# New program orders for all five engines in a fused convolution, attention and expert kernel

## The chip, the cores and the metric

The kernel runs on one core of a Trainium2 chip. The metric is the device time of one execution in microseconds (us). The kernel before took 2512.27 us (median of three runs, 2511.83 to 2513.58).

## What is computed

The input is a batch of 32 images of 56 x 56 positions with 32 channels. Three layers follow each other, each added to its input. The helpers are cut out here.

```python
x = x + conv(group_norm(x))            # batch norm, sign, 3 x 3 convolution with sign(W) * mean|W|
t = tokens(x)                          # 3136 tokens of 32 channels per image
t = t + attention(layer_norm(t))       # 16 heads of 32, linear attention:
    q, k = elu(x Wq + b) + 1, elu(x Wk + b) + 1;  v = x Wv + b
    kv_cos = sum_s k cos(pos) v;  kv_sin = sum_s k sin(pos) v
    qkv = q cos(pos) kv_cos + q sin(pos) kv_sin
    denom = 1 / (q cos(pos) . sum_s k cos(pos) + q sin(pos) . sum_s k sin(pos) + 1e-5)
    out = (qkv * denom) Wdense + b
t = t + experts(layer_norm(t))         # router softmax over 8 experts, the best 2, weighted sum
```

## The kernel before

A prologue (up to about 95 us) loads weights and tables and computes the statistics of the norms over the whole batch. Then the 32 images run through a software pipeline. One image is split into 7 tiles of 4 x 112 positions; each piece of work on a tile or a pair of tiles is a *step*, named by a kind and a number.

Every engine runs its own endless sequence of steps. That sequence isn't derived by the program: it is a table, `ORDER` (line 115), with a list of times for each engine and kind, in units of which `PERIOD = 14` make one image. `iteration` (line 190) sorts all times modulo the period and turns the whole periods into an image offset: a step with time 20.5 is done in iteration i for image i - 1. `walk` (line 216) runs the iterations -3 to B + 2 and calls the engine's `step` function. Only the sorted sequence counts; the numbers themselves play no further part. Each engine takes its steps strictly in this sequence, and steps wait for each other on semaphores.

The steps of one image, with the lines in which the profile shows them:

- **XT**: load (SP, L445), transpose (TensorE L516), sign into `nat` (VectorE L921), residual (ScalarE L663). **CV**: SP copies four shifted versions (L458), convolution (TensorE L525), VectorE L929 adds the residual.
- **XC, SM1, PN1, ZT**: first layer norm. TensorE centres (L530), ScalarE copies and squares (L671, L672), SM1 on VectorE sums the squares (L937) and makes the variance (L940), PN1 on GpSimd takes the power -0.5 and multiplies (L775, L779), TensorE transposes (L537), ScalarE and VectorE split the result into two halves of 16 bits (L679, L951), and SP copies it 16 times into `z` (L465).
- **K** (14 steps): TensorE L546, exponential on ScalarE L683, VectorE L955. **KX** (14): TensorE L555 accumulates keys against positions times values; CS on GpSimd (L787) makes its other operand; KT on ScalarE (L692) and **G** (L564, L696, L701) turn the sum into the matrices for queries.
- **Q** (14): TensorE L571, ScalarE L688, VectorE L961. **DN** (8 steps, VectorE L970 after the 4th and the 8th), **SU** (L588, ScalarE L706), **RC** (VectorE L973, ScalarE L710 and L712), **RL** (VectorE L978): the denominators.
- **R** (7) and **RP** (7): TensorE L597 spreads the denominators; R is multiplied into the queries by VectorE (L983), RP goes through ScalarE (L718) to GpSimd (L792). **NM** (7): TensorE L606, VectorE L989. **T2** (4): TensorE L617 and L619, ScalarE L728 and L730, GpSimd L797.
- **S2, SM2, PN2, ZU**: second layer norm with the same lines as the first (S2: L736 and L945). **LG, RT, GT**: router (TensorE L625, VectorE L993 to L1038, GpSimd L806 to L811). **F** (7): experts, TensorE L631, VectorE L1045, GpSimd L821 to L827. **OUT**: GpSimd L815, store by SP (L472).

PSUM sets how far TensorE may run ahead. K, R, RP, Q, G, LG, F, XC, ZT and ZU share a ring of three slots of two banks (`RING`, `RING_SLOTS = 3`): a step may only start once the step three places before it in TensorE's own sequence has been read. XT, CV, DN, SU, NM and T2 share a single bank (`MISC`), KX has the eighth bank to itself. `rounds` (line 203) works these slots out from TensorE's sequence, so they change with it. The matmuls of K, Q, R and RP write results of 112 or 128 columns, KX, NM and SU of 64, DN and G of 32.

Of the kernel before, what the change touches and what calls it, by code (L numbers as in the profile page):

```python
# [16 lines left out]
G = 4  # L17
# [75 lines left out]
class Img:  # L93
# [10 lines left out]
    def par(self):  # L104
# [9 lines left out]

ORDER = {
    "tensor": {
# [17 lines left out]
    },  # L134
    "vector": {
# [17 lines left out]
    },  # L153
    "scalar": {
# [15 lines left out]
    },  # L170
    "gpsimd": {
        "F": [36.50, 36.53, 37.45, 39.74, 39.75, 42.92, 43.62],
        "PN2": [29.03],
        "RP": [12.84, 15.28, 15.78, 16.42, 17.76, 18.46, 21.18],
        "PN1": [-11.38],
        "CS": [-11.36, -3.38],
        "OUT": [45.32],
        "T2": [18.02, 21.36, 22.75, 26.09],
        "GT": [32.56],
    },  # L180
    "sync": {
        "XT": [-41.70],
        "ZU": [20.02],
        "OUT": [34.22],
        "ZT": [-19.50],
        "CV": [-28.62],
    },
}

# [910 lines left out]
```

How the kernel before makes its waits and increments, by code:

```python
        def wait(eng, s, v):  # L400
            if not isinstance(v, int) or v > 0:
                eng.wait_ge(s, v)
# [10 lines left out]
        @block.sync  # L413
        def _(sp):
            sp.dma_start(eye_center[:, :], eyec).then_inc(eye_in, 16)
            x4 = x.rearrange("(q b) h w c -> q b (h w c)", b=4).rearrange("q b (p f) -> q p b f", p=PT)
            for k in range(2):
                sp.dma_start(stage[k], x4[k]).then_inc(stage_in[k], 16)
            for dst, src in ((mean4_sb[:, :], mean4), (views["rows"], conv_rows),
                             (small[:, 0:1], gamma), (small[:, 1:2], beta), (small[:, 2:3], wd_b)):
                sp.dma_start(dst, src).then_inc(consts_in, 16)
            for q in range(2, 8):
                sp.wait_ge(stage_turned, 4 * q - 4)
                sp.dma_start(stage[q % 2], x4[q]).then_inc(stage_in[q % 2], 16)
            for dst, src in ((views["taps"], conv_taps), (views["valid"], validc), (wva_s, wv[0]), (wvb_s, wv[1]), (wd_s, wd),
                             (views["wqa"], wq[0]), (wqb_s, wq[1]), (views["wka"], wk[0]), (wkb_s, wk[1]),
# [20 lines left out]
            def step(kind, m, n, rd):  # L447
                if kind == "XT" and n == 0:
                    wait(sp, xres_made, m.at(2))
                    load(m)
                if kind == "CV" and n == 0:
                    sp.wait_ge(binarized, m.at(2, 2))
                    for g in range(G):
                        dy, dx = g // 2, g % 2
                        q = slice(32 * g, 32 * g + 32)
```

## Time and profile before

| | |
|---|---|
| median of 3 runs | 2512.27 us |
| the profiled execution, its own time | 2511.5 us |
| its span, first to last instruction | 2509.7 us |
| TensorE busy | 2271.0 us, 90% |
| VectorE busy | 2175.7 us, 87% |
| GpSimd busy | 1745.9 us, 70% |
| ScalarE busy | 1560.4 us, 62% |
| mean granted TensorE clock over the span | 0.964 |

The busy times are unions of the recorded instructions. A busy TensorE isn't a TensorE at its peak, since a matmul's record covers the whole of its passage. The page also follows back the chain of work that ended last: 60% of the span on it is TensorE, 23% VectorE, 9% issue, 3% GpSimd, 2% ScalarE.

### The profile page before, as it was taken

What the parts mean: (1) busy time and instruction counts of PE and PEld (TensorE: products, weight loads), DVE (VectorE), ACT (ScalarE), POOL (GpSimd) and SP (SyncE); (2) the same over time, 40 slices, a digit from 0 to 9 for tenths busy, and PEclk for the clock granted to TensorE, in tenths of its full rate; (3) what the DMA queues carried; (4) which work ended last, traced back from release to release, by engine and by line L of the source; (5) the groups of instructions that cost most, each with busy time, mean ns of one, the idle gap of its engine ahead of it and who ended that gap; (6) DMA issues with size and microseconds to landing.
All of it is one profiled execution on the core that took longest, in us unless ns stands there. A gap on an engine that the chain in (4) does not pass through costs nothing.

```text
span 2509.7 us, 45423 instructions
## 1 busy us (share of the span) xinstructions
PE 2271.0 (90%) x15908; PEld 1106.9 (44%) x15908; DVE 2175.7 (87%) x2949; ACT 1560.4 (62%) x2757; POOL 1745.9 (70%) x1425
## 2 busy tenths in 40 slices
PE   4379999999999999999999999999999999999961
PEld 4224444444444444444444444444444444444441
DVE  5358999999999999999999999999999999999962
ACT  0157666667666666667666666676666666676620
POOL 0414577777777787787777777777777877777675
PEclk8579999999999999999999999999999999999985
DMA  8321111222222112122221111222211111211001
GB/s 221 97 36 21 33 33 32 37 36 43 43 43 38 35 33 36 33 43 43 43 43 33 33 34 35 38 43 43 43 36 34 33 37 34 43 37 34 20 20 26
DMA packets 284863, 105.31 MB, mean 42 GB/s; under 512 B 246032, under 2 KB 279680, under 8 KB 284512
## 3 DMA queue, kind: packets, MB, share of 16 engines
q1 hardware_dynamic: 284640, 102.41, 20.7%
q8 instruction: 131, 2.15, 0.4%
q14 instruction: 92, 0.75, 0.1%
HBM read 31.19 MB, written 12.85 MB: 18 GB/s over the span
## 4 chain that ended last, share of the span: by engine, by line
PE 60%; DVE 23%; issue 9%; POOL 3%; ACT 2%; DMA 2%; SPq 1%; POOLq 0%; DVEq 0%; ACTq 0%
PE ps L555 12%; PE ps L606 10%; PE ps L546 7%; DVE qbuf L961 6%; PE ps L580 6%; PE ps L597 5%; PE ps L571 4%; DVE kbuf L955 4%; PE ps L631 3%; DVE prod L1045 2%; DVE rs L978 2%; DVE qbuf L983 2%; PE ps L530 2%; PE ps L537 2%; PE ps L625 2%
## 5 line engine op out<-in xcount | busy, mean ns | idle before, releaser
L792 POOL TENSOR_TENSOR qbuf<-spread_r,qbuf 128x896 f32<-128x896 f32 x224 | 468.7, 2093 | 335.0 <-ACT spread_r L718 335.0
L683 ACT ACTIVATE ebuf<-ps,small 112x1024 f32<-112x1024 f32 x448 | 499.5, 1115 | 306.4 <-PE ps L546 254.9
L955 DVE SCALAR_TENSOR_TENSOR kbuf<-ps,ebuf 112x1024 f32<-112x1024 f32 x448 | 544.1, 1214 | 78.6 <-ACT ebuf L683 70.4
L688 ACT ACTIVATE ebuf<-ps,small 128x896 f32<-128x896 f32 x448 | 451.8, 1008 | 207.5 <-PE ps L571 149.7
L961 DVE SCALAR_TENSOR_TENSOR qbuf<-ps,ebuf 128x896 f32<-128x896 f32 x448 | 484.8, 1082 | 15.8 <-ACT ebuf L688 14.5
L555 PE MATMUL ps<-kbuf,xcs 112*64 112x512 f32 x1792 | 482.4, 617 | 6.3 <-DVE kbuf L955 6.2
L606 PE MATMUL ps<-qbuf,gmat 128*64 128x224 f32 x3584 | 387.8, 358 | 2.6 <-DVE pbuf L989 2.4
L775 POOL TENSOR_TENSOR rstd<-varr,power 112x28 f32<-112x28 f32 x64 | 307.3, 4802 | 74.9 <-DVE varr L940 71.4
L546 PE MATMUL ps<-wk,z 128*112 128x512 f16 x896 | 284.0, 399 | 54.4 <-DVE qbuf L961 33.6
L606 PEld LDWEIGHTS ps<-qbuf,gmat 128*64 128x64 f32 x3584 | 240.5, 137 | 155.6 <-issue 77.2
L1045 DVE TENSOR_TENSOR prod<-ps,gate 112x1024 f32<-112x1024 f32 x224 | 272.5, 1217 | 22.1 <-POOL ffn L827 12.0
L821 POOL TENSOR_TENSOR prod<-prod 112x512 f32<-112x512 f32 x224 | 285.7, 1275 | 1.4 <-DVE prod L1045 1.4
L571 PE MATMUL ps<-z,wq 128*128 128x448 f16 x896 | 245.8, 356 | 14.5 <-ACT spread_r L718 4.3
L597 PE MATMUL ps<-rs,sel 128*128 128x448 f16 x896 | 241.0, 356 | 17.4 <-DVE kbuf L955 14.8
L983 DVE TENSOR_TENSOR qbuf<-ps,qbuf 128x896 f32<-128x896 f32 x224 | 242.8, 1084 | 9.2 <-PE ps L597 8.9
L718 ACT ACTIVATE spread_r<-ps 128x896 f32<-128x896 f32 x224 | 204.4, 913 | 37.6 <-PE ps L597 32.4
L580 PE MATMUL ps<-qbuf,dmat 128*32 128x448 f32 x1792 | 225.9, 549 | 1.1 <-DVE pbuf L989 1.1
L546 PEld LDWEIGHTS ps<-wk,z 128*112 128x112 f16 x896 | 90.1, 129 | 255.7 <-issue 96.9
L824 POOL TENSOR_TENSOR prod<-prod 112x256 f32<-112x256 f32 x224 | 163.3, 729 | 17.6
L631 PE MATMUL ps<-we,z 128*112 128x256 f16 x896 | 146.0, 288 | 20.1 <-DVE prod L1045 10.2
L555 PEld LDWEIGHTS ps<-kbuf,xcs 112*64 112x64 f32 x1792 | 97.4, 136 | 144.6 <-issue 96.2
L597 PEld LDWEIGHTS ps<-rs,sel 128*128 128x128 f16 x896 | 62.4, 101 | 191.8 <-issue 102.3
(129 smaller groups left out, 3087.1 us busy)
## 6 DMA issues: line engine op xcount, KB each, us to landing
z<-zhl SPq DMA_DIRECT2D x1024, 49.0 KB, 1.9
qbuf<-in_x SPq DMA_DIRECT2D x8, 1568.0 KB, 9.1
xt<-in_x SPq DMA_DIRECT2D x256, 49.0 KB
out<-ffn SPq DMA_DIRECT2D x256, 49.0 KB
shifted<-nat SPq DMA_DIRECT2D x128, 52.6 KB, 5.1
qbuf<-in_sel SPq DMA_DIRECT2D x1, 1024.0 KB, 13.0
tabn<-in_tabnc SPq DMA_DIRECT2D x1, 784.0 KB, 12.7
p<-in_p2c SPq DMA_DIRECT2D x1, 528.0 KB, 9.5
```

The lines of the kernel that those rows point to most:

```text
L546: mm = pe.matmul(o[0:PT, k, :], z1[:, m.par, s % G, s // G, :], wk16[:, :], start=True, stop=True)
L555: mm = pe.matmul(kt_bank[64 * k:64 * k + 64, :], xcs[:, 2 * n + k, :, :].rearrange("p a c -> p (a c)"), kbuf[:, n % 2, DH * k:DH * k + DH] ...
L571: mm = pe.matmul(o[:, k, 0:G * PT].rearrange("p (g t) -> p g t", g=G), wq16[:, 128 * (k0 + k):128 * (k0 + k) + 128], z1[:, m.par, :, j, :] ...
L580: mm = pe.matmul(o[32 * j:32 * j + 32, 0:HW4], dmat[:, m.par, c, :, :].rearrange("p a h -> p (a h)"), qbuf[:, c, 4 * h + j, :], start=(c = ...
L597: mm = pe.matmul(o[:, k, 0:HW4], sel16[:, 128 * a:128 * a + 128], rs[:, j // 4, :], start=True, stop=True)
L606: mm = pe.matmul(o[64 * v:64 * v + 64, 0:2 * PT].rearrange("p (a t) -> p a t", a=2), gmat[:, m.par, c, :, :].rearrange("p a o -> p (a o)") ...
L683: act.activation(ebuf[0:PT, 0, :].rearrange("p (a b) -> p a b", a=2), o[0:PT, :, :], ACT.Exp, bias=minus_one[0:PT, :]).then_inc(kexp_made, 1)
L688: act.activation(ebuf[:, 1, 0:2 * G * PT].rearrange("p (a b) -> p a b", a=2), o[:, :, 0:G * PT], ACT.Exp, bias=minus_one).then_inc(qexp_ma ...
L792: nc.gpsimd.tensor_tensor(qbuf[:, 2:4, n, :], spread_r[:, :, :], qbuf[:, 2:4, n, :], ALU.mult)\
L955: v.scalar_tensor_tensor(kbuf[:, n % 2, :].rearrange("p (a b) -> p a b", a=2), o[0:PT, :, :], 1.0, ebuf[0:PT, 0, :].rearrange("p (a b) -> ...
L961: v.scalar_tensor_tensor(qbuf[:, k0:k0 + 2, j, :], o[:, :, 0:G * PT], 1.0, ebuf[:, 1, 0:2 * G * PT].rearrange("p (a b) -> p a b", a=2), AL ...
L1045: v.tensor_tensor(prod[:, n % 2, :, :].rearrange("p s (e c) -> p (s e) c", c=C), o[0:PT, :, :].rearrange("p k (s c) -> p (k s) c", c=C), g ...
```

## The change

Only the table `ORDER` changes: all 96 steps of TensorE, all of VectorE, ScalarE, GpSimd and SP get new times, and so new places in the sequences. No instruction, tile, buffer or wait of any step is touched. The lists below are the old (-) and new (+) times of TensorE and SP, and of the kinds of VectorE and GpSimd that stand alone; the other lists change in the same way.

```diff
     "tensor": {
-        "R": [12.50, 14.14, 15.05, 16.80, 19.62, 20.52, 23.11],
-        "K": [-4.51, -3.82, -2.49, -2.13, -0.79, -0.30, 0.40, 1.35, 2.10, 3.57, 3.90, 4.43, 4.92, 6.17],
-        "DN": [9.65, 10.29, 10.60, 10.76, 14.46, 14.50, 15.11, 15.23],
-        "F": [36.08, 36.56, 37.43, 38.38, 39.04, 40.45, 42.53],
-        "KX": [-2.70, -2.30, -1.66, -0.91, -0.06, 1.45, 1.85, 2.67, 3.98, 4.55, 4.64, 6.13, 6.38, 7.32],
...
-        "Q": [3.24, 3.80, 4.15, 4.56, 6.12, 6.57, 7.44, 8.71, 9.60, 10.53, 11.21, 11.52, 12.58, 13.31],
-        "NM": [13.90, 17.89, 19.17, 20.18, 20.59, 21.77, 25.86],
...
+        "K": [-6.03, -4.60, -3.25, -1.80, -0.75, 0.18, 1.48, 2.00, 2.47, 2.98, 3.74, 5.01, 5.65, 7.75],
+        "XC": [-13.81],
+        "R": [13.00, 13.21, 14.25, 15.43, 18.80, 20.85, 22.58],
+        "DN": [9.41, 9.71, 10.33, 10.50, 14.66, 14.93, 15.08, 15.31],
+        "F": [36.89, 37.28, 38.52, 39.13, 40.63, 41.95, 42.78],
...
+        "KX": [-3.20, -2.90, -1.50, -0.23, 1.71, 2.17, 2.42, 3.31, 3.78, 5.06, 6.26, 6.59, 7.80, 8.18],
...
+        "Q": [2.25, 2.65, 4.38, 5.36, 6.48, 6.90, 7.96, 8.21, 9.39, 9.65, 10.63, 11.71, 12.38, 13.45],
...
     "vector": {
...
-        "RC": [11.40, 15.88],
-        "RL": [11.97, 16.76],
-        "SM1": [-11.07],
+        "SM1": [-11.66],
+        "RC": [11.71, 17.67],
+        "RL": [12.17, 19.35],
...
     "gpsimd": {
...
-        "PN2": [29.03],
-        "PN1": [-11.38],
+        "PN2": [23.90],
+        "PN1": [-17.45],
...
     "sync": {
-        "XT": [-41.70],
-        "ZU": [20.02],
-        "OUT": [34.22],
-        "ZT": [-19.50],
-        "CV": [-28.62],
+        "CV": [-13.85],
+        "XT": [-27.84],
+        "ZU": [28.91],
+        "ZT": [-9.14],
+        "OUT": [51.80],
```

Sorted, one cycle of TensorE reads as follows; the number in brackets is the image offset, and the last step is followed by the first one of the next iteration.

```
before: R1(-1) K6 DN4(-1) DN5(-1) F6(-3) R2(-1) DN6(-1) DN7(-1) K7 KX5 ZU0(-2) SU1(-1) RP2(-1) KX6 K8 ZU1(-2) XC0(+1) XT0(+2)
  KX7 R3(-1) RP3(-1) Q0 K9 Q1 NM1(-1) K10 KX8 Q2 XT1(+2) K11 KX9 Q3 KX10 K12 NM2(-1) RP4(-1) LG0(-2) R4(-1) ZT0(+1) T20(-1)
  ZT1(+1) Q4 KX11 RP5(-1) K13 NM3(-1) KX12 R5(-1) Q5 NM4(-1) KX13 RP6(-1) Q6 NM5(-1) G0 F0(-2) T21(-1) F1(-2) Q7 G1 T22(-1)
  R6(-1) F2(-2) K0(+1) Q8 DN0 K1(+1) DN1 F3(-2) Q9 DN2 DN3 F4(-2) Q10 KX0(+1) SU0 K2(+1) Q11 KX1(+1) NM6(-1) K3(+1) KX2(+1)
  T23(-1) RP0 F5(-2) R0 CV0(+2) Q12 RP1 KX3(+1) K4(+1) CV1(+2) Q13 K5(+1) NM0 KX4(+1)
after:  K5 XC0(+1) R2(-1) DN4(-1) F6(-3) DN5(-1) DN6(-1) DN7(-1) R3(-1) ZU0(-2) K6 KX4 ZU1(-2) K7 XT0(+2) KX5 Q0 RP2(-1)
  SU1(-1) KX6 K8 Q1 NM1(-1) ZT0(+1) K9 KX7 ZT1(+1) K10 KX8 RP3(-1) Q2 NM2(-1) R4(-1) K11 KX9 Q3 XT1(+2) K12 KX10 Q4 KX11
  LG0(-2) R5(-1) Q5 T20(-1) RP4(-1) K13 KX12 NM3(-1) RP5(-1) Q6 K0(+1) KX13 Q7 NM4(-1) RP6(-1) G0 NM5(-1) R6(-1) G1 F0(-2)
  T21(-1) F1(-2) Q8 K1(+1) DN0 Q9 DN1 DN2 DN3 F2(-2) Q10 K2(+1) KX0(+1) SU0 KX1(+1) F3(-2) Q11 T22(-1) K3(+1) NM6(-1) Q12 RP0
  KX2(+1) F4(-2) T23(-1) R0 RP1 CV0(+2) R1 K4(+1) CV1(+2) Q13 KX3(+1) NM0 F5(-2)
```

VectorE reads most steps in TensorE's sequence. Between them stand its own steps: before, RC1 behind ZU0, RL1 and SM1 between R3 and Q0, RC0 behind Q10 and RL0 behind NM6; after, SM1 between F6 and DN7, RC1 between Q0 and K8, RL1 between ZT1 and K10, RC0 behind K2, RL0 between F3 and Q11. GpSimd's PN2, RP1 and PN1 follow each other directly after the change, with F4 in front and F5 behind. In SP's sequence ZT follows directly on ZU after the change and OUT comes behind it; before, OUT stood between them.

## Rows read from the trace of the kernel before

**Rows 1.** Busy time by stage: length, then busy us (count) of PE, PEld, DVE, ACT, POOL, clock
```profile
900.00:1200.00 300.00, 289.97 (x2045) 137.84 (x2044) 279.03 (x372) 203.04 (x356) 229.89 (x185) 1.00 0.20 36
```

**Rows 2.** Line 625, router matmuls: count, ns min/median/max, first and last start, 300 to 2320 us
```profile
L625 PE MATMUL ps<-we,z x784: 169/193/193, 366.4 to 2289.6; 128*112 128x8 f16 x196
```

**Rows 3.** TensorE's timeline around the longest wait: start, length, instructions [idle before <-releaser]
```profile
1207.89 0.55 PE L571 MATMUL ps<-z,wq 128*128 128x448 f16 x2
1208.56 0.64 PE L546 MATMUL ps<-wk,z 128*112 128x512 f16 x2
...
1209.84 1.74 PE L606 MATMUL ps<-qbuf,gmat 128*64 128x224 f32 x16
1212.56 0.64 PE L546 MATMUL ps<-wk,z 128*112 128x512 f16 x2 [0.99 <-DVE qbuf L961]
```

**Rows 4.** VectorE's timeline in the same stretch
```profile
1207.41 1.09 DVE L983 TENSOR_TENSOR qbuf<-ps,qbuf 128x896 f32<-128x896 f32 x1 [0.26 <-PE ps L597]
1208.54 0.79 DVE L978 TENSOR_TENSOR rs<-den,r_high 64x224 f16<-64x224 f32 x2
...
1210.48 1.03 DVE L940 TENSOR_SCALAR varr<-ssum 112x28 f32<-112x28 f32 x1
1211.43 1.08 DVE L961 SCALAR_TENSOR_TENSOR qbuf<-ps,ebuf 128x896 f32<-128x896 f32 x1
```

**Rows 5.** TensorE's timeline around R0
```profile
1257.31 0.55 PE L597 MATMUL ps<-rs,sel 128*128 128x448 f16 x2 [0.49 <-DVE kbuf L955]
1257.70 0.95 PE L525 MATMUL ps<-shifted,conv_w 128*128 128x448 bf16 x4
1258.48 0.54 PE L571 MATMUL ps<-z,wq 128*128 128x448 f16 x2
```

**Rows 6.** TensorE's timeline, neighbours of equal and of different width
```profile
1228.32 1.03 PE L555 MATMUL ps<-kbuf,xcs 112*64 112x512 f32 x4
1229.29 0.55 PE L597 MATMUL ps<-rs,sel 128*128 128x448 f16 x2
1229.67 0.54 PE L571 MATMUL ps<-z,wq 128*128 128x448 f16 x2
1230.15 1.73 PE L606 MATMUL ps<-qbuf,gmat 128*64 128x224 f32 x16
...
1248.55 1.08 PE L555 MATMUL ps<-kbuf,xcs 112*64 112x512 f32 x4
1249.46 0.55 PE L588 MATMUL ps<-dcs,dsum_sb 128*64 128x224 f32 x4
```

**Rows 7.** VectorE's timeline around R0, and the twin of the variance row
```profile
1257.50 1.21 DVE L1045 TENSOR_TENSOR prod<-ps,gate 112x1024 f32<-112x1024 f32 x1
1258.63 1.08 DVE L983 TENSOR_TENSOR qbuf<-ps,qbuf 128x896 f32<-128x896 f32 x1
1259.63 0.67 DVE L929 SCALAR_TENSOR_TENSOR t<-ps,small,xres 128x448 f32<-128x448 f32 x1
1260.22 0.41 DVE L945 TENSOR_REDUCE ssum<-sq 112x8 f32<-112x256 f32 x1
...
1262.21 0.17 DVE L940 TENSOR_SCALAR varr<-ssum 112x28 f32<-112x28 f32 x1
```

**Rows 8.** One Q step, TensorE's timeline and VectorE's
```profile
1237.68 0.54 PE L571 MATMUL ps<-z,wq 128*128 128x448 f16 x2
...
1239.30 1.09 DVE L961 SCALAR_TENSOR_TENSOR qbuf<-ps,ebuf 128x896 f32<-128x896 f32 x1 [0.20 <-ACT ebuf L688]
```

**Rows 9.** GpSimd's timeline around the variance row
```profile
1209.38 2.10 POOL L792 TENSOR_TENSOR qbuf<-spread_r,qbuf 128x896 f32<-128x896 f32 x1 [4.16 <-ACT spread_r L718]
1211.59 4.80 POOL L775 TENSOR_TENSOR rstd<-varr,power 112x28 f32<-112x28 f32 x1
```

**Rows 10.** SP's timeline, the sixteen copies of one z, and the page's issue row
```profile
1207.18 10.84 SPq L465 DMA_DIRECT2D z<-zhl  x16
...
z<-zhl SPq DMA_DIRECT2D x1024, 49.0 KB, 1.9
```

More of the change, by code:

```diff
@@ L116 @@
     "tensor": {
[17 rows of a table removed]
[17 rows of a table added]
     },
     "vector": {
[17 rows of a table removed]
[17 rows of a table added]
     },
     "scalar": {
[15 rows of a table removed]
[15 rows of a table added]
     },
     "gpsimd": {
-        "F": [36.50, 36.53, 37.45, 39.74, 39.75, 42.92, 43.62],
-        "PN2": [29.03],
-        "RP": [12.84, 15.28, 15.78, 16.42, 17.76, 18.46, 21.18],
-        "PN1": [-11.38],
[L176 to L179, printed above, removed]
+        "RP": [6.87, 10.24, 11.16, 12.55, 15.18, 15.92, 16.13],
+        "T2": [15.86, 16.53, 17.97, 21.34],
+        "GT": [30.06],
+        "F": [31.08, 31.54, 31.74, 32.94, 35.59, 38.79, 40.65],
+        "CS": [-15.39, -10.87],
+        "PN2": [23.90],
+        "PN1": [-17.45],
+        "OUT": [41.93],
     },
     "sync": {
-        "XT": [-41.70],
-        "ZU": [20.02],
-        "OUT": [34.22],
-        "ZT": [-19.50],
-        "CV": [-28.62],
+        "CV": [-13.85],
[3 more added lines that the diff above has]
+        "OUT": [51.80],
     },
```

78 rows, old and new, of the table ORDER are left out of this document.

## The prediction

> **What bounds the kernel now.** Read the stages first, as busy time per 300 us stretch [rows 1]: TensorE is busy 290.0 of 300 us, VectorE 279.0, ScalarE 203.0, GpSimd 229.9, at a granted clock of 1.00 (the 2.4 GHz level). Two engines are nearly full, and neither is full. Next, the period. The row of the router matmuls [rows 2] holds 28 images of 28 matmuls; from the first start (366.4) to the last (2289.6), less the 1.4 us inside the last image, there are 27 periods: 71.2 us per image.
>
> How much of the 71.2 us is TensorE work? Going through the 96 steps of one image in the TensorE timeline, I took each step from its first start to the next step's first start, at the smallest value that this pair of neighbours has anywhere in the steady part. The sums: 14 KX 13.7, 7 NM 11.3, 14 K 7.3, 8 DN 7.1, 14 Q 6.3, 7 R and 7 RP 5.9, 4 T2 4.3, 7 F 3.2, the other 14 steps 8.8; together 67.8 us. So TensorE stands still for 71.2 - 67.8 = 3.4 us per image. The same sum for VectorE is 64.6.
>
> Where it stands still shows in [rows 3]: Q0, K9 and NM1 start at 1207.89, 1208.56 and 1209.84 (Q1 between the last two), and K10 only at 1212.56, with "DVE qbuf" as releaser. An NM takes 1.6, so 1.1 us is lost in front of K10 alone and 2.0 us in the stretch. The other side is [rows 4]: in that time VectorE reads R3 (1207.41), makes RL1 (two instructions from 1208.54), SM1 (until 1211.43, its variance row alone 1.03 us), and only then reads Q0 (until 1212.51). Only three slots of PSUM (the ring) stand between the engines: K10 needs the slot that Q0 held. TensorE had 3.0 us of work there, VectorE 5.0. The next largest loss is at R0, whose slot K3 held: 0.49 us of idle in its row [rows 5], 0.65 from start to start. Most TensorE time lost is of this kind: a run of VectorE work in the wrong place, longer than three slots cover.
>
> **The change, part by part.** No instruction is added or removed; only positions move. So both work sums stay, save for neighbours on TensorE.
>
> *Narrow runs.* A switch between results of 128 or 112 columns (K, Q, R) and of 64 or 32 (KX, NM, SU, DN, G) has a price in [rows 6]: R before Q takes 0.38, Q before NM 0.48, so entering costs 0.1; KX before R 0.97, KX before SU 0.91, so leaving costs 0.06 (0.1 before a K). Going round the cycle, the old order changes width 49 times and the new one 47 times: 0.2 us. With every other pair of neighbours at its old price, and pairs that the old order does not have at the nearest one (SU before KX as SU before K less one exit; DN5 before DN6 as DN6 before DN7), the new sum is 67.2; if each unknown pair takes the dearer of its nearest prices it is 67.75, no gain. I take 67.5: 0.3 us per image.
>
> *Where VectorE's long pieces stand.* SM1 moves from between RL1 and Q0 to between F6 and DN7, RL1 to behind ZT1, RC1 to between Q0 and K8, XC0 on TensorE to directly behind K5. Laid side by side with the waits left out, VectorE's start of reading behind TensorE's end of writing swings over 5.9 us within an image in the old order (4.75 at Q1, -1.18 at R6), and over 4.1 in the new one (7.55 to 3.42, another origin). Three slots cover about 3 us of it, and an average slope of 3 us per image (67.5 against 64.6) VectorE absorbs by idling. So the 2.0 us stretch goes. What is late next, worked through the new cycle from step to step:
> - CV1 waits for the one misc bank, which CV0 holds. TensorE from F4 to CV1: F4 0.5, T23 0.67, R0 0.39, RP1 0.39, CV0 0.78 [rows 5], R1 0.39, K4 0.48 = 3.6. VectorE from the same F4: 0.6 until it can start (the 1.62 of [rows 8] less an exponential of 1.0), F4 1.13, R0 1.00, CV0 0.59 [rows 7], S22 0.33, 0.05 to the release [rows 3, 4] = 3.7, and it comes 0.35 late out of Q12: 0.45 us of wait.
> - RP0 waits for the slot of Q11. TensorE from Q10's start: Q10, K2, KX0, SU0, KX1, F3, Q11, T22, K3, NM6, Q12 by the sums above 7.9. VectorE: 1.62 from a Q's start to its reading [rows 8], Q10 1.0, K2 1.13, RC0 1.46, F3 1.13, RL0 0.75, Q11 1.0, 0.05 = 8.15: 0.25 us.
> - K9, R4, K1 and K4 come out within 0.1 us of their slots.
> That makes 0.7 us. Worked the same way, the old order gives 2.8 of the 3.4 us seen, since ScalarE's strict order and handovers are counted short; I add the missing 0.5. Between 0.7 (nothing missed) and 2.6 (ScalarE's strict order: RC1, RC0 and KT0 stand directly in front of the exponentials of K10, K3 and Q7 and delay each by up to 1 us, of which two thirds would reach TensorE) I take 1.2, since the old order's error is the nearest row.
>
> *SM1's price.* Its variance row takes 1.03 while the GpSimd multiply RP3 runs (1209.38 + 2.10 = 1211.48; the row ends at 1211.51), the twin of SM2 takes 0.17 with GpSimd idle [rows 4, 7, 9]. In the new place RP1 is the GpSimd step before PN1. From SM2 to SM1's variance VectorE has K4, Q13, NM0, F5, K5, R2, F6 and the sum of squares = 8.0 plus its idling of more than 1; PN2 and RP1 take 6.6 + 2.1 = 8.7. So the variance row falls just behind RP1: 0.2 rather than 1.03. It lies on VectorE alone, which has slack there; at the other end, up to 2.1 us, ZU1, K7 and RP2 wait 0.8 us for their slots. The 1.2 above holds for 0.2, and 2.0 is inside the end of 2.6.
> The Trainium skill (SBUF — State Buffer, section "Who interferes with whom") says that VectorE and GpSimd share a pair of ports, that the one that issues first holds it for its whole instruction, and that the other blocks. The 1.03 us row agrees. By that rule the place of SM1 can also cost: rival 4.
>
> *Queues.* SP issues the 16 copies of one z in 10.84 us [rows 10], and the page's landing is 1.9. Today the output copies lie between ZU's and ZT's; the new order puts ZT directly behind ZU. From ZU1's start on TensorE to the landing of ZT: about 2.4 until VectorE has it, 10.84 + 10.84 + 1.9 = 26.0 us. TensorE has 26.8 us of work from ZU1 to K0 of the next image, and its waits: hidden by 0.8 us, and each us over that is a us at K0. LG waits for ZU's copies alone (15 of 19 us). Output, CV and XT follow and have 20 us or more. GpSimd (229.9 of 300) gets PN2, RP1, PN1 in a row; PN1 ends near 13 us after K5, ZT0 needs it at 15.6: hidden by 2.6.
>
> *Ends.* From an image's K0 to its output step the new program is 3.9 periods long instead of 3.7, 8 us more at the end; from XT0 to K0 it is 11 us shorter at the start. I take them as even, +-8 us.
>
> **The sum.** Period 67.5 + 1.2 = 68.7 against 71.2: 2.5 us per image; over the 28 images of the constant period 70 us. The profiled execution ran 2511.5 us (span 2509.7), and the median of the runs shown is 2512.3, 0.8 above. 2511.5 - 70 = 2441.5, and about 0.8 for the median: 2442. I say 2445, for the small handovers that no row prices.
>
> **The rivals.**
> 1. Half the gain: ScalarE's order costs its 2.6 us, so the period is 70.1 and the time 2512 - 28 x 1.1 = 2481 (2466 to 2492). For it: ScalarE takes K, RC and Q in strict order, and XC0 is the longest block; against: it is busy only 203 of 300 us.
> 2. Only the narrow runs count: waits move, none disappears. Period 70.9 to 71.1, time 2503 to 2509. For it: two switches in 49 is all that the change's name stands for; against: the 2.0 us stretch has lost its cause. By its named effect alone the change would do almost nothing.
> 3. Slower: the z copies on SP. If ZT's landing comes more than 3.7 us behind its place (30.5 us of chain instead of 26.8; 16 us for a set of copies would do it), K0 makes the period longer than 71.2; one us beyond that is 2512 + 28 = 2540. For it: 0.8 us of slack where 2.5 stand today; against: both sets take 10.84 to within 0.01 us, and VectorE reads ZU1 with nothing long in front.
> 4. SM1 under the power op: GpSimd begins PN2 3 us late, behind the sums of F4, and SM1's variance row is held until the power op (4.80 us [rows 9]) ends; of that TensorE, with 0.8 us of lead, waits some 4.0: period 72.7, time 2512 + 28 x 1.5 = 2554. For it: the variance row in [rows 4] waited like that for a shorter op; against: F4's sums end before SM2 if the order runs as worked out. (The skill's rule named above is this mechanism.)
>
> **How the numbers follow.** Forecast (2425 to 2465) 0.61; below 2425 0.04; rival 1 0.22; rival 2 0.06; rival 3 0.05; rival 4 0.02. The range goes from 2420 (period 67.9, the 0.7 us of waits with 67.2 of work) to the top of rival 1, 2492, and leaves out under 0.2. A difference of 0.2% (5 us) is about what a measurement of this kernel can tell from no change. Rival 2 falls half on each side of that bound: faster 0.90, same 0.03, slower 0.07.
>
> **What would show it.** Right: the router row's starts 68.7 us apart; busy time of TensorE above 295 of 300; the K10 row without a VectorE releaser; the variance row of SM1 near 0.2 us; the largest TensorE waits in front of CV1 and RP0. Wrong: a K0 that waits for the z copies (rival 3), a variance row of 2 to 5 us (rival 4), idle time in front of K with ScalarE as the last step (rival 1), or a work sum above 67.8, which would mean that switches between 64 and 32 wide cost more than I took.

## The result, and the profile after

The changed kernel takes 2550.26 us (median, 2548.13 to 2552.29), the kernel before 2512.28: a ratio of 1.015 with a 95% interval of 1.0133 to 1.0168. It is slower by 38 us, where 67 us less were forecast. Its profiled execution has a span of 2546.3 us.

A stage of the changed kernel, to be read against [rows 1] (busy us of PE, PEld, DVE, ACT, POOL), and the router matmuls of 28 images, against [rows 2]:

```profile
900.00:1200.00 300.00, 279.03 (x2007) 137.12 (x2006) 288.30 (x362) 198.34 (x358) 223.58 (x184) 1.00 0.19 36
```

```profile
L625 PE MATMUL ps<-we,z x784: 192/193/213, 359.6 to 2327.0; 128*112 128x8 f16 x196
```

The period is (2327.0 - 1.4 - 359.6) / 27 = 72.8 us instead of 71.2. TensorE is busy for 11 us less of the 300, and VectorE, whose work was not changed, for 9 us more. So some VectorE instructions became longer. The sum of TensorE's steps without waits, worked as in the prediction, is 67.9 in this trace (67.8 before), so by it TensorE now stands still for 4.9 us per image (3.4 before). Some of the 67.9 is itself standing still, as the account of the narrow runs below shows.

The stretch on which the forecast was built did what was foretold. TensorE's timeline around K10, answering to [rows 3] (K9, ZT1, K10):

```profile
1221.84 0.60 PE L546 MATMUL ps<-wk,z 128*112 128x512 f16 x2
...
1223.38 0.51 PE L537 MATMUL ps<-eye_center,xn 112*128 112x112 f32 x3
1223.72 0.60 PE L546 MATMUL ps<-wk,z 128*112 128x512 f16 x2
```

K10 has no releaser any more. VectorE's timeline at SM1, answering to [rows 4], and GpSimd's RP1:

```profile
1210.52 1.08 DVE L937 TENSOR_REDUCE ssum<-sq 112x28 f32<-112x896 f32 x1
1211.63 0.18 DVE L940 TENSOR_SCALAR varr<-ssum 112x28 f32<-112x28 f32 x1
```

```profile
1209.57 2.10 POOL L792 TENSOR_TENSOR qbuf<-spread_r,qbuf 128x896 f32<-128x896 f32 x1
```

The variance row takes 0.18 us, as worked out. It begins 0.04 us ahead of the end of RP1 (1209.57 + 2.10 = 1211.67), where the prediction had it just behind. The time is lost elsewhere. The costliest idle time of TensorE on the page after (group of the R and RP matmuls: busy, mean ns, idle before them and what ended it):

```profile
L597 PE MATMUL ps<-rs,sel 128*128 128x448 f16 x896 | 241.7, 357 | 111.1 <-DVE qbuf L961 110.0
```

That is 3.5 us per image in front of RP5, RP6 and RP0. VectorE's timeline ahead of RP5 and RP6, where the router steps RT2 (L1025, L1027), RT3 (L1014, L1016) and RT4 stand:

```profile
1238.25 0.39 DVE L1025 TENSOR_TENSOR route<-route,rmax 112x224 f32<-112x224 f32 x1
1238.68 2.17 DVE L1027 SCALAR_TENSOR_TENSOR route<-route 112x224 f32<-112x224 f32 x1
1240.77 1.08 DVE L961 SCALAR_TENSOR_TENSOR qbuf<-ps,ebuf 128x896 f32<-128x896 f32 x1
...
1243.19 0.37 DVE L1014 TENSOR_REDUCE rmax<-route 112x28 f32<-112x224 f32 x1
1243.60 2.23 DVE L1016 TENSOR_TENSOR route<-route,rmax 112x224 f32<-112x224 f32 x1
1245.86 0.39 DVE L1020 TENSOR_TENSOR route<-route,first 112x224 f32<-112x224 f32 x1
```

GpSimd's timeline in the same time (RP4, T20, RP5):

```profile
1238.51 2.09 POOL L792 TENSOR_TENSOR qbuf<-spread_r,qbuf 128x896 f32<-128x896 f32 x1 [1.61 <-ACT spread_r L718]
1240.56 0.76 POOL L797 TENSOR_TENSOR xc<-t,mean 112x256 f32<-112x256 f32 x1
1243.48 2.10 POOL L792 TENSOR_TENSOR qbuf<-spread_r,qbuf 128x896 f32<-128x896 f32 x1 [2.17 <-ACT spread_r L718]
```

And TensorE's (RP5, then RP6 and G0):

```profile
1241.90 0.55 PE L597 MATMUL ps<-rs,sel 128*128 128x448 f16 x2 [1.47 <-DVE qbuf L961]
...
1247.73 0.55 PE L597 MATMUL ps<-rs,sel 128*128 128x448 f16 x2 [0.91 <-DVE qbuf L961]
1248.86 0.32 PE L564 MATMUL ps<-p,ktsb 128*32 128x66 f32 x8 [0.58 <-DVE kbuf L955]
```

Read the three together. Two VectorE instructions on 224 elements take 2.17 and 2.23 us, and each ends 0.25 us behind the end of a GpSimd multiply (1240.85 against 1240.60, 1245.83 against 1245.58). Instructions of the same shape right beside them take 0.39. In the kernel before, GpSimd stood still in these moments; VectorE's timeline there (the second instruction of RT2 and of RT3) and GpSimd's:

```profile
1226.78 0.39 DVE L1027 SCALAR_TENSOR_TENSOR route<-route 112x224 f32<-112x224 f32 x1
...
1228.50 0.39 DVE L1016 TENSOR_TENSOR route<-route,rmax 112x224 f32<-112x224 f32 x1
```

```profile
1224.80 0.70 POOL L797 TENSOR_TENSOR xc<-t,mean 112x256 f32<-112x256 f32 x1 [0.67 <-ACT mean L730]
1229.17 2.10 POOL L792 TENSOR_TENSOR qbuf<-spread_r,qbuf 128x896 f32<-128x896 f32 x1 [3.67 <-ACT spread_r L718]
```

A third place is RL0, whose two instructions together take 1.77 us beside GpSimd's sum of F3, as against 0.79 for RL1 in [rows 4]; RP0 then waits 1.24 us. VectorE, then GpSimd, then TensorE, after:

```profile
1265.70 1.77 DVE L978 TENSOR_TENSOR rs<-den,r_high 64x224 f16<-64x224 f32 x2
```

```profile
1265.80 1.43 POOL L821 TENSOR_TENSOR prod<-prod 112x512 f32<-112x512 f32 x1
```

```profile
1268.65 0.55 PE L597 MATMUL ps<-rs,sel 128*128 128x448 f16 x2 [1.24 <-DVE qbuf L961]
```

Together 1.8 + 1.8 + 1.0 = 4.6 us of VectorE per image.

### The profile page after: what moved, and what is told of

Read it like the earlier page. It is cut to its first block, busy times and chain, and to the rows that moved or that the text cites. A ratio compares the mean times of both kernels' runs of the same rounds, so it can differ in the third digit from the quotient of the medians.

```text
span 2546.3 us, 45423 instructions
## 1 busy us (share of the span) xinstructions
PE 2241.0 (88%) x15908; PEld 1115.7 (44%) x15908; DVE 2286.5 (90%) x2949; ACT 1542.2 (61%) x2757; POOL 1752.3 (69%) x1425
## 4 chain that ended last, share of the span: by engine, by line
PE 44%; DVE 32%; issue 11%; POOL 5%; ACT 4%; DMA 2%; SPq 1%; POOLq 0%; ACTq 0%; DVEq 0%
PE ps L555 9%; PE ps L580 8%; DVE qbuf L961 7%; DVE kbuf L955 6%; PE ps L606 6%; PE ps L546 4%; PE ps L571 4%; DVE prod L1045 4%; DVE route L1016 3%; ACT ebuf L683 3%; PE ps L597 3%; PE ps L625 2%; PE ps L631 2%; PE ps L530 2%; DVE den L973 2%
## 5 line engine op out<-in xcount | busy, mean ns | idle before, releaser
L546 PE MATMUL ps<-wk,z 128*112 128x512 f16 x896 | 275.9, 390 | 22.7 <-issue 12.1
L571 PE MATMUL ps<-z,wq 128*128 128x448 f16 x896 | 245.4, 355 | 2.5 <-DVE qbuf L961 1.3
L580 PE MATMUL ps<-qbuf,dmat 128*32 128x448 f32 x1792 | 218.1, 545 | 0.3 <-DVE pbuf L989 0.3
L679 ACT ACTIVATE zhl<-ps 128x448 f16<-128x448 f32 (+1 forms) x128 | 63.6, 498 | 166.9 <-PE ps L537 166.9
```

Of the source, the lines that this page charges most:

```text
L546: mm = pe.matmul(o[0:PT, k, :], z1[:, m.par, s % G, s // G, :], wk16[:, :], start=True, stop=True)
L571: mm = pe.matmul(o[:, k, 0:G * PT].rearrange("p (g t) -> p g t", g=G), wq16[:, 128 * (k0 + k):128 * (k0 + k) + 128], z1[:, m.par, :, j, :] ...
L580: mm = pe.matmul(o[32 * j:32 * j + 32, 0:HW4], dmat[:, m.par, c, :, :].rearrange("p a h -> p (a h)"), qbuf[:, c, 4 * h + j, :], start=(c = ...
```

## The experiments

Three theories stood against each other. *Port theory*: a VectorE instruction that reads both inputs from SBUF is held while a GpSimd instruction runs, and the new orders lay three of them under GpSimd. *Order theory*: VectorE's row of router steps is too long where it stands, whatever GpSimd does. *TensorE theory*: the new order of TensorE costs the time itself.

### GpSimd made to wait, orders kept

The sharpest test gives an engine that is off the path more to wait for: by the port theory the kernel becomes faster, by the others it can't. The added lines (`step` of GpSimd; the first run has the first two, the second run the last two, the third run all):

```diff
                 elif kind == "RP":
                     pool.wait_ge(r_copied, m.at(7, n + 1))
+                    if n in (4, 5) and m.c >= 1:
+                        pool.wait_ge(route_step, m.at(16, -9 if n == 4 else -6))
...
                 elif kind == "F":
                     pool.wait_ge(prod_made, m.at(7, n + 1))
+                    if n == 3 and m.c + 2 < B:
+                        pool.wait_ge(r_made, m.at(2, 5))
```

> The changed kernel with two waits added on GpSimd and nothing else: its multiply RP4 begins only when VectorE's RT2 of the image before is done, RP5 only when the first instruction of RT4 is. All orders stay. Port theory (a VectorE instruction with two SBUF inputs is held while a GpSimd instruction runs): the second instruction of RT2 and of RT3 fall from 2.17 and 2.23 us to about 0.4, VectorE gains 3.6 us per image, and TensorE's waits in front of RP5 (1.26), K0 (0.36), RP6 (0.74) and G0 (0.58) go: 2.9 us per image, 2550 - 28 x 2.9 = 2469 us (2455 to 2490). Rival, order theory (VectorE's row of router steps is too long by its place, whatever GpSimd does): the rows stay or the waits do, GpSimd is only later: 2550 or up to 20 us slower. Rival, TensorE theory (the narrow runs themselves cost the time): 2550.

Measured: 2452.82 us, ratio to the kernel before 0.9757 (0.9743 to 0.9772), period 69.5: 3.3 us per image where 2.9 were expected, and 2 us below the range.

> The changed kernel with one wait added on GpSimd and nothing else: its sums of F3 begin only when VectorE's RL0 is done. Port theory: the second instruction of RL0 falls from 1.37 us to about 0.4, Q11 is read 1.0 us earlier and the 1.40 us wait of RP0 falls to about 0.4: 1 us per image, 2550 - 28 = 2520 us (2515 to 2540). Order theory (RP0 waits since RC0, F3, RL0 and Q11 stand in a row on VectorE): 2550, since GpSimd only begins later.

Measured: 2521.75 us, 1.0036 (1.0022 to 1.0049), period 71.8; RL0's second instruction 0.39 us instead of 1.37.

> The changed kernel with all three added waits on GpSimd (RP4 behind RT2, RP5 behind RT4's first instruction, F3's sums behind RL0). Port theory: both gains, 2550 - 28 x 3.9 = 2441 us (2430 to 2475), which is the time that was forecast for the change. If the two gains share a slack, nearer 2470. Order theory and TensorE theory: 2550 or slower.

Measured: 2420.63 us, 0.9635 (0.9619 to 0.9651), period 68.5, faster than both kernels. It lies 9 us below the expected range: 4.3 us per image were gained instead of 3.9, and in more than the 28 periods that were reckoned. VectorE's timeline of this run at the same steps (RT2, Q5, K13, then RT3):

```profile
1183.69 0.39 DVE L1031 SCALAR_TENSOR_TENSOR route<-route 112x224 f32<-112x224 f32 x1
1184.00 1.08 DVE L965 SCALAR_TENSOR_TENSOR qbuf<-ps,ebuf 128x896 f32<-128x896 f32 x1
1185.00 1.21 DVE L959 SCALAR_TENSOR_TENSOR kbuf<-ps,ebuf 112x1024 f32<-112x1024 f32 x1
...
1186.83 0.39 DVE L1020 TENSOR_TENSOR route<-route,rmax 112x224 f32<-112x224 f32 x1
```

GpSimd's, now released by VectorE (RP4, RP5):

```profile
1184.22 2.09 POOL L794 TENSOR_TENSOR qbuf<-spread_r,qbuf 128x896 f32<-128x896 f32 x1 [2.31 <-DVE route L1031]
...
1187.79 2.10 POOL L794 TENSOR_TENSOR qbuf<-spread_r,qbuf 128x896 f32<-128x896 f32 x1 [0.91 <-DVE route L1024]
```

TensorE's (RP5, without a wait), and what is left of TensorE's waits in 1200 us (what waited <- for what: us, times, longest):

```profile
1185.38 0.55 PE L597 MATMUL ps<-rs,sel 128*128 128x448 f16 x2
```

```profile
PE ps L525 <- DVE t L933: 4.8, 17, 0.3
PE ps L597 <- DVE qbuf L965: 4.3, 17, 0.3
```

The held rows are back at 0.39, and RP5 starts at once. The gains add up: 3.3 us per image from the router steps, 1.0 from RL0, 4.3 together, and the order and TensorE theories, which foresaw no gain, are out. Beside RP4, which runs from 1184.22 to 1186.31, Q5 and K13 take their usual 1.08 and 1.21: they read one input from PSUM. Only the rows with both inputs in SBUF are held here. This isn't the whole rule: SM1's variance row [rows 4] has a single input, in SBUF, and was held too.

### The router steps moved instead

Without any wait, VectorE's table alone (RT2 behind NM3; RT3, RT4 and RT5 behind NM4):

```diff
-        "RT": [35.21, 35.39, 35.49, 36.13, 36.75, 37.16, 38.10],
+        "RT": [35.21, 35.39, 35.935, 37.12, 37.14, 37.60, 38.10],
```

> The changed kernel with only VectorE's order changed: RT2 behind NM3, and RT3, RT4, RT5 behind NM4, so that they fall into the times in which GpSimd has nothing to do (RP4 and RP5 then run beside Q5, K13, Q6 and K0, which read PSUM). No wait is added. Port theory: RT2 and RT3 run at 0.4 us per instruction, the waits of RP5, K0, RP6 and G0 shrink by 2 to 2.9 us per image: 2470 us (2460 to 2495). TensorE theory: 2550.

Measured: 2489.2 us, 0.9906 (0.9892 to 0.9921), period 70.7, inside the expected range. RT2's first instruction still takes 0.52 us under the end of T20 and RL0 is held as in the changed kernel, but RT2's and RT3's long rows are gone. So the same cause is removed in two ways. This one gives some back: three router steps (RT3, RT4, RT5) now stand in a row, and R6 on TensorE waits 1.08 us for the slot of the Q step behind them.

### What a switch of width costs

Both runs start from the kernel with the three waits, which TensorE bounds almost alone, and move single steps in TensorE's table. The first breaks up five runs of narrow results (the table sorted):

```diff
- Q13 KX3 NM0 ... SU0 KX1 F3 ... SU1 KX6 K8 ... DN6 DN7 R3 ... DN2 DN3 F2
+ KX3 Q13 NM0 ... SU0 F3 KX1 ... SU1 K8 KX6 ... DN6 R3 DN7 ... DN2 F2 DN3
```

> The kernel with the three GpSimd waits (2420.6 us, period 68.5 with 67.9 of TensorE work), and on TensorE alone five steps moved by one place so that five runs of narrow results are broken up: Q13 behind KX3, F3 behind SU0, K8 behind SU1, R3 behind DN6, F2 behind DN2. Ten more switches of width per image, 57 instead of 47. Switch-price theory (0.06 to 0.1 us each, from pairs of neighbours): TensorE's work sum rises by 0.6 to 1.0 us, 2437 to 2449 us. Rival (a switch costs nothing; the neighbours' differences are something else): 2420, work sum unchanged. If the moves make new waits, these show in front of KX, DN or NM with VectorE as releaser, and the work sum tells them apart.

Measured: 2462.44 us, 0.9803 (0.9787 to 0.982), period 69.8 instead of 68.5. It lies above both expectations. TensorE's waits in 1200 us are those of the kernel with the three waits to within 0.5 us. So the 1.3 us are work: 0.13 us for each of ten switches, more than the 0.06 to 0.1 read from pairs. The price is real and a switch is dearer than was taken.

The second brings narrow results together at three places:

```diff
- KX13 Q7 NM4 ... KX10 Q4 KX11 ... NM5 R6 G1
+ Q7 KX13 NM4 ... Q4 KX10 KX11 ... NM5 G1 R6
```

> The kernel with the three GpSimd waits, and on TensorE alone three steps moved by one place so that narrow results come together: Q7 ahead of KX13, Q4 ahead of KX10, R6 behind G1. Six switches fewer per image, 41 instead of 47. Switch-price theory: work sum lower by 0.36 to 0.6 us, 2404 to 2411 us. Rival (a switch costs nothing): 2420. If KX10 now holds VectorE's K12, or R6 comes late, part is given back: 2410 to 2425 with the work sum lower all the same.

Measured: 2432.54 us, 0.9685 (0.9671 to 0.9699), period 68.8: 12 us slower than the kernel it starts from, and outside all that was expected. TensorE's waits in the same 1200 us:

```profile
PE ps L571 <- ACT spread_r L718: 8.4, 17, 0.8
PE ps L525 <- DVE t L933: 5.1, 18, 0.3
PE ps L571 <- DVE kbuf L959: 4.5, 17, 0.5
PE ps L597 <- DVE qbuf L965: 4.3, 17, 0.3
```

Two waits are new, those of Q steps (L571) that now stand one place earlier: 12.9 us in some 17.4 images, 0.74 us per image. The period rose by 0.3 only, so the work fell by 0.44: 0.07 us for each of six switches. The switches were saved and more was paid for them in ring slots.

Neither run tells width from type: every narrow result of this kernel is fp32, and K, Q, R and F are fp16. The traces can. TensorE of the changed kernel (KX7 and ZT1, Q5 and T20, KX12 and NM3):

```profile
1222.37 1.08 PE L555 MATMUL ps<-kbuf,xcs 112*64 112x512 f32 x4
1223.38 0.51 PE L537 MATMUL ps<-eye_center,xn 112*128 112x112 f32 x3
...
1235.36 0.54 PE L571 MATMUL ps<-z,wq 128*128 128x448 f16 x2
1235.74 0.39 PE L617 MATMUL ps<-eye_mean,t1b 128*112 128x132 f32 x2
...
1237.84 1.08 PE L555 MATMUL ps<-kbuf,xcs 112*64 112x512 f32 x4
1238.74 1.69 PE L606 MATMUL ps<-qbuf,gmat 128*64 128x224 f32 x16
```

ZT and T2 are fp32 with wide results (128 and 112 columns). KX takes 1.01 us before ZT, which changes the width alone, and 0.90 before NM, which changes nothing. Q takes 0.38 before T2, which changes the type alone, as R does before Q in [rows 6]. So the price goes with the width.

### SM1 and the router steps in the old order

Is the old order, but for SM1's row, nearly free of such rows by chance, and what is SM1's place worth by itself? All five runs here start from the kernel before. First, GpSimd's RP3 waits for SM1's variance row:

```diff
                     pool.wait_ge(r_copied, m.at(7, n + 1))
+                    if n == 3 and m.c + 2 < B:
+                        pool.wait_ge(var_made[0], m.at(1, 3))
```

> The kernel before, with one wait added on GpSimd and nothing else: RP3 begins only when the variance row of VectorE's SM1 is done. It tests the step on SM1 by itself. Port theory: the variance row falls from 1.03 to 0.17 us, Q0 is read 0.86 us earlier, the wait of K10 falls from 1.1 to 0.25 us, period 71.2 to 70.35: 2513 - 24 = 2489 us (2485 to 2500). Rival (K10 is late by the length of the whole row R3, RL1, SM1, Q0, and what is gained there is waited for again at the next long piece): 2505 to 2513. Rival (GpSimd, 1.2 us later with PN1, becomes the bound): over 2513, with waits on xn or qbuf from GpSimd.

Measured: 2523.96 us, 1.005 (1.0035 to 1.0065), period 71.7. The variance row is 0.18 us, and yet the kernel is slower. VectorE at RT0, then GpSimd at RP4:

```profile
1231.26 0.38 DVE L1016 TENSOR_REDUCE rmax<-route 112x28 f32<-112x224 f32 x1
1231.67 1.87 DVE L1018 TENSOR_TENSOR route<-route,rmax 112x224 f32<-112x224 f32 x1
```

```profile
1231.20 2.08 POOL L794 TENSOR_TENSOR qbuf<-spread_r,qbuf 128x896 f32<-128x896 f32 x1
```

RP3's wait made PN1, CS0, OUT and RP4 about 2 us later in the cycle: RP4 began 2.19 us ahead of RT0 in the kernel before (1222.04 and 1224.23) and begins 0.06 us ahead here, so it fell on RT0, which it had just missed. 0.85 us were saved at SM1; at RT0 1.48 were lost in the image shown and 1.33 in the mean of sixteen. None of the three expectations had named this; it is the port theory at a step that none of them weighed.

Second, on VectorE, SM1 behind Q0 instead of ahead of it (`"SM1": [-11.07]` becomes `[-10.875]`).

> The kernel before with one step moved on VectorE: SM1 behind Q0 instead of ahead of it. Q0 is read at once, so K10's wait of 1.1 us goes, and SM1's variance row falls behind RP3's end: 0.17 us. If nothing else happens the period falls from 71.2 to about 70.1: 2512 - 31 = 2481 us. Port theory says that something else happens: GpSimd's PN1 starts 0.7 us later in the cycle and all behind it with it, VectorE is 1 us earlier, and so RT0's second instruction, which ran 0.1 us behind RP4's end in the kernel before, comes while RP4 runs: held to 1.4 to 1.9 us instead of 0.39, most of the gain lost: 2500 to 2525 us. Order theory: 2481.

Measured: 2518.06 us, 1.0027 (1.0015 to 1.004), period 71.4. RT0's second instruction takes 0.74 us, held for less than expected. K10's wait is gone, but the Q step behind it waits 0.6 us and K11 0.5.

Third, RT3 behind K13 (`34.21` becomes `34.935` in `"RT"`), under RP5.

> The kernel before with one step moved on VectorE: RT3 behind K13, where GpSimd's RP5 is running (it began after RT3 before). Port theory: RT3's second instruction takes 1.2 to 1.7 us instead of 0.39, RT3's first one (a maximum along rows, one input) and K13 keep their time; VectorE has 0.9 us of idle in front of NM5 to take it up, so 0 to 0.6 us per image: 2512 to 2530 us. Order theory: all rows keep their time and the kernel 2512 within 5.

Measured: 2548.18 us, 1.0149 (1.0134 to 1.0165), period 72.4. VectorE at RT3, then GpSimd at RP5:

```profile
1246.30 0.38 DVE L1014 TENSOR_REDUCE rmax<-route 112x28 f32<-112x224 f32 x1
1246.71 1.12 DVE L1016 TENSOR_TENSOR route<-route,rmax 112x224 f32<-112x224 f32 x1
```

```profile
1245.49 2.10 POOL L792 TENSOR_TENSOR qbuf<-spread_r,qbuf 128x896 f32<-128x896 f32 x1 [3.67 <-ACT spread_r L718]
```

The two VectorE rows read the same 224 columns, one after the other, both under RP5. The maximum, which has one input, takes its 0.38; the comparison, which has two in SBUF, is held until 0.24 us behind RP5's end. The size of the row was as expected, a little short. The time was not: moving RT3 together with its 0.73 us of hold costs 1.2 us per image, not up to 0.6. The idle in front of NM5 didn't take it up.

Fourth, SM1 behind Q0 and RT0 behind ZT1 (`33.23` becomes `33.555` in `"RT"`).

> The kernel before with two steps moved on VectorE: SM1 behind Q0, and RT0 behind ZT1, so that RT0's second instruction comes when RP4 has ended. Port theory: no row held (variance 0.17, RT0's second instruction 0.4 to 0.8 us), K10's wait gone, period 70.0 to 70.6: 2478 to 2495 us, faster than the same kernel with SM1 alone moved. Order theory: as with SM1 alone or slower, since the router steps only come later.

Measured: 2587.16 us, 1.0304 (1.0289 to 1.0319), period 73.8, where 2478 to 2495 was expected. RT0's row is 0.39, but RT3, later with RT0, fell under RP5. VectorE, GpSimd, and TensorE's NM4 behind:

```profile
1263.66 2.15 DVE L1016 TENSOR_TENSOR route<-route,rmax 112x224 f32<-112x224 f32 x1
```

```profile
1263.48 2.08 POOL L792 TENSOR_TENSOR qbuf<-spread_r,qbuf 128x896 f32<-128x896 f32 x1 [3.46 <-ACT spread_r L718]
```

```profile
1266.16 1.74 PE L606 MATMUL ps<-qbuf,gmat 128*64 128x224 f32 x16 [1.63 <-DVE pbuf L989]
```

Fifth, the same with one wait added on GpSimd, RP5 behind RT3 (`if n == 5 and m.c >= 1: pool.wait_ge(route_step, m.at(16, -7))`).

> The kernel before with SM1 behind Q0 and RT0 behind ZT1 on VectorE (2587 us as it stood, RT3's second instruction 2.15 us under RP5, period 73.8), and GpSimd's RP5 now waits until RT3 is done. Port theory: RT3's second instruction 0.39 us, RP5 0.5 us later, NM3 is read 1.8 us earlier and the 1.6 us wait of the NM behind it goes: period 71.2 to 72.0, 2505 to 2535 us, 50 us or more below the kernel without the wait. It also tells what SM1's place is worth in the old order with no row held: if the 2.0 us stretch were simply gone, 70.2 and 2480; if what was gained in front of K10 is waited for at the next steps (a Q behind K9 waits 0.6 us in the last runs), 71.2 and 2510. Order theory: 2587, since GpSimd only begins later.

Measured: 2537.67 us, 1.0093 (1.0076 to 1.011), period 72.1: 49 us less than without the wait, just short of the 50 expected, and 3 us outside its range. Neither the variance row nor a router row is held in this kernel (one row of RL is, by 0.16), and it is still slower than before: the Q step behind K10 waits 0.6 us, K11 0.5, two steps that follow an expert step on VectorE 0.7 in sum, and R0 0.5 as before. So SM1's place behind Q0 gains nothing in the old order.

## Why the prediction was wrong

- **What bounds the kernel** was read rightly. TensorE's waits come from VectorE's long pieces in the wrong place, and K10's stretch vanished.
- **The failing step is "Where VectorE's long pieces stand".** The walk through the new cycle, with its swing of 4.1 us, gave VectorE's steps their old durations: RL0 has "0.75", and RT2 and RT3 (0.39 per instruction before) put none of RP5, RP6 and G0, which now wait, among its late steps. Those durations hold only while GpSimd doesn't hold the row. The prediction knew the mechanism: under "SM1's price" it explained the 1.03 us row by RP3, and rival 4 was a slower kernel by just this. But it looked for it at one step, the one that [rows 4] shows held. GpSimd's new sequence was never laid in time beside VectorE's other instructions with two SBUF inputs, the thirteen of RT and RL. At up to 2.1 us each [rows 9] the three overlaps would have stood in the sum as some 4.6 us of VectorE; the runs show that 4.3 of it reach TensorE (72.8 - 68.5).
- **With the holds taken away the sum was right**: period 68.5 against 68.7, and TensorE's two largest waits are those named, CV1 (0.28, forecast 0.45) and RP0 (0.25, forecast 0.25). The forecast had 67.5 of work and 1.2 of standing still; by the same working this run has 67.2 and 1.3, of which 0.6 show as waits in the profile.
- **Narrow runs**: 0.3 us were taken, and about as much came. The 67.9 of the changed kernel seems to say that none did, but in its trace some pairs of neighbours never meet without a wait: NM before RP takes 1.90 us at the least, and 1.62 in the run with all waits, where TensorE has the same sequence. In that run's trace the sum is 67.2, and by the same working 67.5 for the kernel before, whose 67.8 held 0.27 us of waiting (F4 behind DN3). The price per switch is of the size taken (0.07 and 0.13 measured). Of the prediction's 49 and 47 switches one each lies between 64 and 32 columns; between wide and narrow results there are 48 and 46, and the difference of two, worth 0.14 to 0.26, stands. Rival 2's reading, that the change's named effect is next to nothing, was right, its time wrong.
- **SM1's price** fell to 0.18 as worked out, but with luck: the row began 0.04 us ahead of RP1's end, and the working was not that fine. **Queues** held: K0 doesn't wait for the z copies (rival 3). Rival 4 named the right mechanism at the wrong place, and its 2554 lies close to the 2550 by coincidence. Rival 1 is out: ScalarE ends no large wait.
- **Ends** were taken as even within 8 us. In the run with all waits the first router step is 7.5 us earlier than before (287.7 against 295.2 us), and the sum's 28 periods should have been 31, since the last images gain as well: 31 x 2.7 + 7.5 = 91 us of the 92 measured. The sum had 28 x 2.7 = 76: this term alone was 15 us short.

Open stays what each of the new orders is worth on its own. In the old order SM1 behind Q0 gains nothing, with or without a held row, and its new place between F6 and DN7 was not tried there; in the new order all moves together bring 2.7 us per image once the three holds are gone.

## What to carry to other kernels

When an order moves, lay GpSimd's instructions in time beside every VectorE instruction that reads both inputs from SBUF, and beside short rows like SM1's variance row, and charge each overlap the rest of the GpSimd instruction, not a few per cent. Look for the signature in a trace: a short VectorE row whose end falls just behind the end of a GpSimd row. The cure can be a wait on the engine that has slack: making GpSimd wait at three places took 130 us off this kernel.

## What the runs showed of the hardware

The hold lasts until the other instruction ends: 0.39 us became 2.23 when the VectorE instruction came just behind the start of a multiply of 2.10, and 1.12 when it came 1.2 us behind the start. In the thirteen traces 645 rows of RT and RL with both inputs in SBUF begin with more than 0.15 us of a GpSimd instruction to go, beside its multiplies, sums and subtractions alike. Every one of them ends 0.24 to 0.26 us behind the end of that instruction.

Which instruction is held depends on where its inputs lie, but not on that alone. With both inputs in SBUF it is held; with one of them in PSUM (Q 1.08, K 1.21) it isn't. Of those with a single input in SBUF, a reduction (0.38) isn't, nor is RC's reciprocal (1.54 with and without GpSimd), but SM1's variance row, a TENSOR_SCALAR, is: 1.03 under RP3, and 0.18 where RP3 was made to wait. 101 such rows in the traces end 0.03 to 0.04 us behind the GpSimd instruction.

The Trainium skill (SBUF — State Buffer, section "Who interferes with whom") says that a VectorE instruction with two SBUF inputs contends with a GpSimd instruction that reads SBUF, and that a reduction never does on this chip. The rows above agree (2.23 against 0.38), and the prediction used only the half of the section that fitted SM1.

GpSimd paid little where it came second: its sum in F3 took 1.43 us behind RL0's first instruction, 1.27 without.
